# Head of a gated cross-attention kernel: the first norm in two halves, a bank for each transposed tile, one of four copies on VectorE

## What is computed

```
x = x + tanh(g_xattn) * attention(layernorm(x), ctx, ctx, Wq, Wk, Wv, Wd)   # 32 heads, 8 key/value groups, dk = 128, causal
x = x + tanh(g_ffn)   * (layernorm(x) @ dequantize(qweight).T + bias)
layernorm(x) = (x - mean) / sqrt(var + 1e-5)
```

## Time and profile before

| | |
|---|---|
| median of 3 runs | 1047.81 us (1047.72 to 1048.31) |
| the profiled execution's own time | 1048.74 us |
| its span (first to last instruction) | 1046.9 us |
| PE busy | 1007.0 us, 96% of the span |
| DVE, ACT, POOL busy | 720.9, 500.6, 288.4 us |
| PE in the first of 40 equal slices of the span | 40 to 50% busy; nearly all later slices 90% or more |
| start of the first query product | 20.81 us after the start of the span |

### The profile page before, as it was taken

One profiled execution on the slowest core, in us unless ns is written; L12 is line 12 of the kernel. 1 busy time (PEld: TensorE's weight loads), 2 busy tenths in 40 slices (PEclk: granted clock), 3 DMA queues, 4 the chain that ended last, 5 costly groups with the idle time before them and its releaser, 6 DMA issues.

```text
span 1046.9 us, 21306 instructions
## 1 busy us (share of the span) xinstructions
PE 1007.0 (96%) x8130; PEld 598.3 (57%) x8130; DVE 720.9 (69%) x1486; ACT 500.6 (48%) x1033; POOL 288.4 (28%) x285
## 2 busy tenths in 40 slices
PE   4889999999999999999999999999999999999995
PEld 2555555555555555555555555555567776776742
DVE  5856777677586676865667667665667766666778
ACT  5777676675633343334543434344454444444422
POOL 1364664465714001412210503143000120000013
PEclk9999999999999999999999999999999999999997
DMA  7648546434473542455544775146754454533211
GB/s 281 211 156 299 194 155 215 164 101 163 130 262 136 153 95 101 159 156 178 208 169 165 234 216 172 25 160 182 218 173 157 133 172 145 183 127 122 81 36 60
DMA packets 97523, 168.65 MB, mean 161 GB/s; under 512 B 35472, under 2 KB 68240, under 8 KB 83728
## 3 DMA queue, kind: packets, MB, share of 16 engines
q1 hardware_dynamic: 97424, 167.30, 49.3%
HBM read 110.89 MB, written 33.55 MB: 138 GB/s over the span
## 4 chain that ended last, share of the span: by engine, by line
PE 84%; DVE 10%; ACT 3%; issue 2%; DMA 1%; SPq 0%; DVEq 0%; ACTq 0%
PE pa L1708 33%; PE py L1708 30%; PE av L1887 5%; PE pa L1783 4%; PE av L1783 3%; PE pp L1865 3%; PE ps L1849 2%; PE py L1945 2%; PE pp L1849 2%; DVE q L1209 2%; DVE sc L1305 1%; DVE row_max L1303 1%; DVE sc L1299 1%; DVE sc L1316 1%; DVE wq L1209 1%
## 5 line engine op out<-in xcount | busy, mean ns | idle before, releaser
L1708 PE MATMUL py<-wd,att 128*128 128x512 f16 x1488 | 337.5, 379 | 1.7 <-DVE att L1329 0.9
L1708 PE MATMUL pa<-xT,wq 128*128 128x512 f16 x1152 | 257.2, 379 | 10.1 <-DVE q L1209 7.8
L1708 PEld LDWEIGHTS py<-wd,att 128*128 128x128 f16 x1488 | 143.3, 98 | 158.4 <-issue 2.6
L1708 PEld LDWEIGHTS pa<-xT,wq 128*128 128x128 f16 x1152 | 109.3, 98 | 145.2 <-issue 19.3
L1338 DVE SCALAR_TENSOR_TENSOR xacc<-py,f_y,xacc 128x512 f32<-128x512 f32 x128 | 95.6, 747 | 91.3 <-PE py L1708 91.3
L934 ACT ACTIVATE att<-av 128x256 f16<-128x256 f32 x256 | 80.8, 384 | 135.7 <-PE av L1887 135.3
L883 ACT ACTIVATE q<-pa 128x512 f16<-128x512 f32 x96 | 56.8, 591 | 171.4 <-PE pa L1708 171.4
L1329 DVE SCALAR_TENSOR_TENSOR att<-av,att 128x256 f16<-128x256 f32 x256 | 93.3, 417 | 65.6 <-ACT att L934 65.3
L1708 PE MATMUL pa<-wv,cT 128*128 128x128 f16 x1536 | 96.2, 219 | 0.0
L1708 PEld LDWEIGHTS pa<-wv,cT 128*128 128x128 f16 x1536 | 89.8, 98 | 0.9
L1209 DVE SCALAR_TENSOR_TENSOR q<-pa,q 128x512 f16<-128x512 f32 x96 | 65.8, 685 | 35.3 <-ACT q L883 33.5
(11 more groups left out here) (180 smaller groups left out, 1400.8 us busy)
## 6 DMA issues: line engine op xcount, KB each, us to landing
wq<-kept_q SPq DMA_DIRECT2D x24, 1024.0 KB, 8.8
wd<-kept_d SPq DMA_DIRECT2D x23, 1024.0 KB, 6.1
v_dup<-v_nat SPq DMA_DIRECT2D x128, 128.0 KB, 2.4
raw_d<-in_wdT SPq DMA_DIRECT2D x8, 1024.0 KB, 10.0
kept_q<-wq SPq DMA_DIRECT2D x8, 1024.0 KB, 9.2
kept_d<-wd SPq DMA_DIRECT2D x8, 1024.0 KB, 5.2
raw_d<-in_wqT SPq DMA_DIRECT2D x8, 1024.0 KB, 7.1
raw_q<-in_wqT SPq DMA_DIRECT2D x7, 1024.0 KB, 5.3
```

Of the source, the lines that this page charges most:

```text
L1708: last = pe.matmul(out, stationary(a, i), moving(b, i), start=(i == 0 and (a, b) == PASSES[0]), stop=(i == count - 1 and (a, b) == PASSES[ ...
```

## The change

- The norm of block 0 is made in two pairs of tiles: statistics, guess, refinement and normalisation of tiles 0 and 1 come first, then the same for tiles 2 and 3.
- ACT makes the HI parts of tiles 0 and 1 ahead of the squares of the query weights, copies tiles 0 and 1 out, and only then makes the HI parts of tiles 2 and 3.
- POOL writes the LO parts of tiles 0, 1 and 2; DVE that of tile 3 alone.
- PE transposes tiles 0 and 1 between the first `warm_up` and `weight_norms(0, 0, 2)`, tiles 2 and 3 after the second `warm_up`. Since the guess of the first pair now makes seed_ok 4, the first `warm_up` is released by that pair.
- Tiles 2 and 3 are transposed into banks py0 and py1, so that none of the four shares a bank.
- The copy of tile 3 from its bank to xT is DVE's, placed after `high` of the second head and ahead of that head's `split_wq`.
- Counts of seed_ok and rsd_ok are moved to fit (`seeds`, and 20 and 30 for 10 and 20 at the end of the kernel).

```diff
-DVE_LO = (1, 3, 28, 29, 30, 31)
+DVE_LO = (3, 28, 29, 30, 31)
...
+        def seeds(call):
+
+            return 4 * call + (4 if call > 0 else 0)
+
+        def transpose_bank(t):
+
+            return py[t % 2] if t in (2, 3) else av[t % 2]
...
 # POOL
-                pool.wait_ge(seed_ok, 4 * (call + 1))
+                pool.wait_ge(seed_ok, seeds(call) + 4)
...
-            ln_lo(0)
-            ln_lo(2)
+            for t in range(TILES - 1):
+                ln_lo(t)
             ctx_lo(0, range(KC - len(C0_DVE)))
...
 # ACT, the copy of a tile
                 act.copy(xT[:, par, :, :, at:at + P],
-                         av[t % 2][:, :].bitcast(F16).rearrange("p (c k n) -> p c k n", c=2, k=KC)).then_inc(xT_ok, 1)
+                         transpose_bank(t)[:, :].bitcast(F16).rearrange("p (c k n) -> p c k n", c=2,
+                                                                        k=KC)).then_inc(xT_ok, 1)
...
+            ln_hi(0, False)
+            ln_hi(1, False)
             squares_q(0, 0)
             squares_q(0, 1)
-            for t in range(TILES):
-                ln_hi(t, False)
-            for t in range(TILES):
-                ln_out(t)
+            ln_out(0)
+            ln_out(1)
+            ln_hi(2, False)
+            ln_hi(3, False)
+            ln_out(2)
             ctx_squares(0, 2)
...
 # DVE
+            def ln_out(t):
+
+                dve.wait_ge(xT_mm, tile_count(t) + 1)
+                at = t % TILES * P
+                dve.tensor_copy(xT[:, 0, :, :, at:at + P],
+                                transpose_bank(t)[:, :].bitcast(F16).rearrange("p (c k n) -> p c k n", c=2,
+                                                                               k=KC)).then_inc(xT_ok, 1)
...
-            for t in range(TILES):
-                ln_bn(0, t)
-            ln_stats(0)
-            dve.wait_ge(seed_ok, 4)
-            rstd_here(0, slice(0, TILES))
-            for t in range(TILES):
-                ln_norm(t)
+            for pair in (0, 2):
+                ln_bn(0, pair)
+                ln_bn(0, pair + 1)
+                ln_stats_of(0, pair)
+                rstd_here(5 * pair, slice(pair, pair + 2))
+                ln_norm(pair)
+                ln_norm(pair + 1)
             weight_scale(0, slice(0, 1))
             dve.wait_ge(w_mul_ok, 1)
             high(wq[:, 0, HI, 0, :, :], raw_q[:, 0, 0, :, :], w_mul[:, 0, 0:1], wq_hi)
-            ln_lo(1)
             split_wq(0, 0)
             ln_lo(3)
             for h in range(1, HPG):
                 high(wq[:, 0, HI, h, :, :], raw_q[:, 0, h, :, :], w_mul[:, 0, 0:1], wq_hi)
+                if h == 1:
+                    ln_out(3)
                 split_wq(0, h)
...
 # PE
-                bank16 = av[t % 2][:, :].bitcast(F16)
+                bank16 = transpose_bank(t)[:, :].bitcast(F16)
...
             warm_up(WARM_UP[0])
+            ln_transpose(0, 0)
+            ln_transpose(1, 0)
             weight_norms(0, 0, 2)
             pe.wait_ge(w_exp_ok, 1)
             warm_up(WARM_UP[1])
-            for t in range(TILES):
-                ln_transpose(t, 0)
+            ln_transpose(2, 0)
+            ln_transpose(3, 0)
             q_unit(0, 0)
```

More of the change, by code:

```diff
@@ L1358, in ln_stats @@
                 dve.tensor_scalar(half_var[:, :], mv[:, :, 1], LN_EPS, -0.5, ALU.add, ALU.mult).then_inc(seed_ok, 1)
-                dve.wait_ge(seed_ok, 4 * call + 2)
+                dve.wait_ge(seed_ok, seeds(call) + 2)
                 dve.tensor_scalar(rs_bits[:, :], var_e[:, :].bitcast(I32), 1, None,
                                   ALU.logical_shift_right).then_inc(seed_ok, 1)
-                dve.wait_ge(seed_ok, 4 * call + 3)
+                dve.wait_ge(seed_ok, seeds(call) + 3)
                 dve.tensor_scalar(rs[:, 0, :].bitcast(I32), rs_bits[:, :], -1.0, float(RSQRT_MAGIC),
@@ L1366, in ln_stats_of @@
             def ln_stats_of(call, pair):
-                before = 4 * call + 2 * pair
+                before = seeds(call) + 2 * pair
                 two = slice(pair, pair + 2)
@@ L1674, in _ @@
             ln_stats_of(last, 0)
-            rstd_here(10, slice(0, 2))
+            rstd_here(20, slice(0, 2))
             ln_norm(TILES * last)
@@ L1684, in _ @@
             ln_stats_of(last, 2)
-            rstd_here(20, slice(2, 4))
+            rstd_here(30, slice(2, 4))
             ln_norm(TILES * last + 2)
```

## The result

The changed kernel takes 1050.46 us as the median of 20 runs (1049.31 to 1051.35), the kernel before 1048.86 (1047.72 to 1051.65, 20 runs). The ratio is 1.0015 with a 95% interval of 1.0009 to 1.0021: 1.6 us slower, where 0.86 us less was forecast, and outside the range that was given. The forecast named the mechanism that decided, as its first rival, the late clock, and took its price as nothing. The forecast counts from a median of 3 runs, 1047.81; with 20 runs that kernel stands at 1048.86, so 1.05 us of the distance between 1047.0 and 1050.46 lies in that base.

A forecast was written before the change was run, and what follows sets the result against it. PE was taken to bound the kernel, so an earlier first query product pulls the rest: 20.81 to 19.95 gains 0.86, clock costs 0. 1047.81 - 0.86 = 1046.95, stated as 1047.0 us, range 1045.5 to 1049.2.

The forecast's parts named there:

- the late clock: Rival at the first query product: PE's clock rises only within it, 0.3 to 1.4 us slower overall; chance 0.27.
- I take 0, the rise falling before 19.95: Clock term at the first query product: PE reaches 2.4 GHz before it starts, so no added time.
- The upper bound that I gave, 2.3: Extra us if the first query product's twelve matmuls run wholly at 1.2 GHz, 5.0 for 2.75 us.
- First pair: Head, tiles 0 and 1: normalisation from 7.56, POOL from 8.92 to about 11.2, beside the squares, costing nothing.
- Second pair: Head, tiles 2 and 3: rs_bits held by POOL to 11.2, normalisation at 13.60, query-weight scale at 14.53, 0.55 later.
- To the first product: Head, from scale through held split, tile 3's LO part, transposes and 1.23 us DVE copy: first query product at 19.95.
- my lower bound: DVE's copy of tile 3 from PSUM: 0.69 us if two fp16 elements pass together.
- The sum: First query product's start moves from 20.81 to 19.95, a gain of 0.86 us.
- The end: Rival at the last products, partly at half clock: 2.3 us less or about 1.1 more; chance 0.06 for over a microsecond.
- the late clock with a slow end: Clock rise within the first query product plus slower last products: over 1049.9 us, reaching 1050 at worst; chance 0.07.
- Costed at nothing: Head: earlier first warm-up, ctx_squares at about 18.5, later DVE splits and a weight load 2 us later, all free.
- the upper end that the forecast had tied to transposes that do not raise the clock: Whole first query product slow because transposes do not count as clock activity: 1049.3 us; chance 0.08.

The follow-up runs named there:

- experiment 1: Changed kernel plus three unused warm-up products, one between the transposes of tiles 2 and 3, two behind them; 1047.72 us, 0.9989 to the kernel before.
- experiment 3: Changed kernel with the separate banks and DVE copy undone, keeping the norm in halves; 1049.76 us, ratio 1.0012 to the kernel before.
- experiment 4: Kernel before without its second warm-up of three unused products; 1050.21 us, ratio 1.0009 to the kernel before.
- experiment 7: Changed kernel with three unused warm-up products and tile 1's LO part back on DVE; 1048.08 us, ratio 0.9990 to the kernel before.
- when filled: Changed kernel with six extra warm-up products in the head and 17 in PE's waits at the end; 1046.17 us, ratio 0.9976 to the kernel before.
- further executions 2 and 4: Two of four more profiled executions of the kernel before, code unchanged; the first query product took 4.44 us in each.

## Why the prediction was wrong

The step that failed is the sentence "I take 0, the rise falling before 19.95, since the stretch of work is nearly as long as before". The term measured 2.53 us in both profiles of the changed kernel, and experiments 1, 3 and 4 show that this is the cause: filling the holes of PE brings 2.0 of it back with DVE's work unchanged, the halves alone have it, and the old order gets it when its warm-up is taken away. The upper bound that I gave, 2.3, was nearly right as a size. The choice between the bounds was not, and its own rows gave reason to doubt it. In the profile before, PE had worked from 14.18 with one hole of 0.34 us, and the level rose at 19.05, 4.9 us later. The new order was forecast to work from 14.7 to 18.56, 3.9 us, and then to rest 1.4. In the event it worked from 14.84 to 18.94 with a hole of 0.66 us between the transposes of tiles 2 and 3, rested 0.87, and the level had not risen.

Point by point:

- *First pair*: first normalisation at 7.64 (7.56 forecast), POOL on tiles 0 and 1 from 9.01 (8.92). Right.
- *Second pair*: one operation was held to the end of POOL's part, as forecast, though half_var (1.13 for 0.16) and not rs_bits; normalisation at 13.72 (13.60), scale at 14.63 (14.53). Right, and experiment 7 confirms the holder.
- *To the first product*: `high` was held (1.43 for 0.48), where the forecast had put the hold on the split behind it; the split ran free, tile 3's LO part ended at 17.82 for 17.25. Against that, DVE's copy took 0.69, which was my lower bound; I had taken 1.23. The Trainium skill, "VectorE: DVE Perf Modes", section "The perf-mode tier table", was right for this copy: up to twice the plain rate, an estimate of 0.65 against 0.69 measured. The start at 19.81 (19.95 forecast) is therefore luck in part: 0.4 too late in DVE's work and 0.5 too early in the copy offset each other.
- *The sum*: 1.00 gained at the start in the profiled pair, 0.86 forecast. But the old start of 20.81 was the latest of five executions. Their mean is 20.0, that of the changed kernel's two 19.86, so the usual gain at the start is about 0.15 us. This is the second fault: I read one execution's arrival of a load as the kernel's own. Against the mean of the old order the changed kernel thus gains 0.15 at the start and loses 1.6 by the product's length (5.28 for a mean of 3.68).
- *The end*: its last 16 matmuls took 5.36 to 6.53 us in all profiled executions but two (4.90 in the second execution of the changed kernel, 3.61 when filled). They move the time by about a microsecond from execution to execution, of one kernel as well (6.53 and 4.90), so they are not what separates the two kernels.
- *The range and its chances*: the range was given as 1045.5 to 1049.2, but its chance of 0.77 was counted between 1045.7 and 1049.9. The time lies above both, where the forecast had put 0.07 for the late clock with a slow end. The late clock came at its full price; the rest of the distance is the base of 1047.81, not the end.
- *Costed at nothing*: ctx_squares at 18.21, the context's scale at 25.69 behind the product, the load behind the splits at 22.79. None of them was waited for.

The length of the product came out at the upper end that the forecast had tied to transposes that do not raise the clock, 2.53 for 2.3. In experiment 4, 32 transposes without a warm-up before them left the product at 1.2 GHz but for its very end (5.17 for 5.28 us); those transposes had holes of 0.9 and 0.3 us too. In the profile before, and in further executions 2 and 4, the level rose in the midst of transposes (in the latter two sixteen took 1.62 and 1.61 us, where at the low level they take 1.91). The Trainium skill, "TensorE: Matmul & The Clock Gate", section "Part 4: PE-mode transpose", says that transposes do not count as activity for the clock in the way that products do. Experiment 4 fits this and the three rises rather do not; no run here has transposes alone without holes, so it stays open. Open stays also why the level rises in time, or falls again, in some executions of the same kernel and not in others.

## What to carry to other kernels

Moving early work of TensorE forward can cost more than it gains when it breaks up the stretch of work ahead of the first long product; read the length of that product, not only its start, and fill the holes with products that nothing uses (here 2.7 us for three of them). A level that is up can be lost again in the rest before the product, so the last hole counts too. Before pricing a change in a kernel's head, profile several executions: the first product's start moved by 1.4 us and its length by 1.7 with no change in the code. A bound that decides the sign of a forecast should not be taken at its good end because the pattern looks "nearly" the same.

## What was not expected of the hardware

- The granted clock's column read 1.00 while twelve matmuls ran at 1.2 GHz (632 ns each): ahead of the first change of level it holds no reading. The instruction lengths tell the level there.
- In two of five executions of the kernel before, the granted clock fell to a half 0.3 us into the first product, after a rest of 1.22 us and transposes at the high level (0.61 us for eight).
- Some kinds of DVE operation were held beside POOL's LO parts, others not. Held: half_var (1.13 us for 0.16, ending with POOL's part), `high` (1.43 for 0.48, ending 0.3 behind it), an LO part (1.30 for 0.68, ending 0.5 behind it). Free beside POOL's in the same stretch: the statistics (1.28 for two) and the aggregation of tiles 2 and 3 (0.30 for two).
- DVE copied 128x1024 fp16 values from PSUM in 0.69 us, ACT in 1.01.
